# Seven block products for the queries of two cross attentions, and a value product ahead of the scores

## The reference, cut to what matters

```python
def _cross_attention(q_in, kv_in, wq, bq, wk, bk, wv, bv, wo, bo, bias_k, bias_v):
    qh = (q_in @ wq + bq).reshape(b, q_len, H, K)
    kh = (kv_in @ wk + bk).reshape(b, t, H, K)
    vh = (kv_in @ wv + bv).reshape(b, t, H, K)
    kh = jnp.concatenate([kh, broadcast(bias_k)], axis=1)
    vh = jnp.concatenate([vh, broadcast(bias_v)], axis=1)
    logits = jnp.einsum('bqhk,bthk->bhqt', qh, kh) / jnp.sqrt(K)
    weights = jax.nn.softmax(logits, axis=-1)
    ctx = jnp.einsum('bhqt,bthk->bqhk', weights, vh).reshape(b, q_len, H * K)
    return ctx @ wo + bo
# x = x + attention 1 of layer_norm(x); x = x + attention 2 of layer_norm(x); then an MLP
```

## Time and profile before

| | us |
|---|---|
| median of 3 runs | 1042.86 |
| lowest, highest | 1041.63, 1045.31 |
| the profiled execution | 1042.48 |
| its span (first to last instruction) | 1041.3 |

### The profile page before, as it was taken

How to read it: one execution, slowest core, us unless ns; L and a number is a source line. 1 busy time by engine, 2 the same in 40 slices (tenths; PEclk the granted TensorE clock), 3 DMA queues, 4 the chain that set the end, 5 groups by cost and what they waited for, 6 DMA issues and landing times.

```text
span 1041.3 us, 21141 instructions
## 1 busy us (share of the span) xinstructions
PE 1003.6 (96%) x8239; PEld 902.9 (87%) x8239; DVE 768.8 (74%) x1229; ACT 577.5 (55%) x1288; POOL 651.5 (63%) x595
## 2 busy tenths in 40 slices
PE   8899999999999999999998999999998999989998
PEld 7788888888988999999997999999998888777877
DVE  7997888998265677877668876778875387898760
ACT  5998888797533323232233322213225489999982
POOL 6885476655577475344367566655535388999960
PEclk9999999999999999999999999999999999999999
DMA  8200001000121211221121111101120000000000
GB/s 335 110 2 2 1 2 42 2 1 2 47 76 42 71 35 58 71 82 42 41 76 30 41 42 41 31 19 33 31 102 1 1 1 2 2 2 2 12 11 21
DMA packets 33931, 40.73 MB, mean 39 GB/s; under 512 B 2127, under 2 KB 31273, under 8 KB 32297
## 3 DMA queue, kind: packets, MB, share of 16 engines
q1 hardware_dynamic: 33833, 39.38, 11.3%
HBM read 38.32 MB, written 1.05 MB: 38 GB/s over the span
## 4 chain that ended last, share of the span: by engine, by line
PE 79%; POOL 9%; DVE 5%; ACT 4%; issue 1%; DMA 1%; SPq 0%; DVEq 0%; ACTq 0%; POOLq 0%
PE psum L912 10%; PE psum L791 9%; PE psum L807 9%; PE psum L992 8%; PE psum L944 8%; PE psum L926 6%; PE psum L979 5%; PE psum L958 5%; PE psum L833 5%; POOL C tile L1789 3%; PE psum L718 3%; PE psum L968 3%; PE psum L823 3%; PE psum L848 2%; POOL C tile L1795 2%; PE psum L862 1%
## 5 line engine op out<-in xcount | busy, mean ns | idle before, releaser
L1926 POOL TENSOR_TENSOR B tile<-B tile,B rec 128x1024 f32<-128x1024 f32 x32 | 61.1, 1908 | 164.5 <-DVE B rec L1348 164.5
L1795 POOL TENSOR_TENSOR A tile<-A tile,outer rec 128x1024 f32<-128x1024 f32 x48 | 91.0, 1905 | 57.9 <-DVE outer rec L1187 57.8
L1652 ACT COPY B PT<-psum 128x512 f32<-128x512 f32 x64 | 32.9, 600 | 140.7 <-PE psum L968 140.7
L1069 DVE TENSOR_SCALAR B qT<-psum,cols 128x1024 f32<-128x1024 f32 (+1 forms) x38 | 44.0, 1166 | 78.0 <-PE psum L912 76.6
L1567 ACT ACTIVATE A tile<-A tile,outer min 128x128 f32<-128x128 f32 (+1 forms) x256 | 92.3, 448 | 2.6 <-DVE outer min L1180 2.5
L1567 ACT ACTIVATE C tile<-C tile,outer min 128x128 f32<-128x128 f32 x256 | 77.8, 396 | 0.5 <-DVE outer min L1180 0.4
L944 PE MATMUL psum<-B v hi,cT hi 128*128 128x256 f32 x256 | 72.1, 282 | 0.3 <-ACT B kT L1482 0.3
L944 PE MATMUL psum<-B v hi,cT lo 128*128 128x256 f32 x256 | 71.6, 280 | 0.0
L944 PE MATMUL psum<-B v lo,cT hi 128*128 128x256 f32 x256 | 71.6, 280 | 0.0
L1795 POOL TENSOR_TENSOR C tile<-C tile,outer rec 128x1024 f32<-128x1024 f32 x32 | 60.8, 1906 | 6.1 <-DVE outer rec L1187 6.1
L1173 DVE TENSOR_TENSOR A tile<-m,psum 128x1024 f32<-128x1024 f32 x48 | 56.5, 1216 | 9.2 <-PE psum L823 8.0
(11 more groups left out here) (327 smaller groups left out, 3474.8 us busy)
## 6 DMA issues: line engine op xcount, KB each, us to landing
weights<-in_weights_c SPq DMA_DIRECT2D x5, 1024.0 KB, 6.4
raw<-in_wq SPq DMA_DIRECT2D x32, 128.0 KB, 2.7
raw<-in_wk SPq DMA_DIRECT2D x32, 128.0 KB, 3.2
raw<-in_wv SPq DMA_DIRECT2D x16, 256.0 KB, 2.8
raw<-in_wo SPq DMA_DIRECT2D x16, 256.0 KB, 2.7
weights<-in_weights_a SPq DMA_DIRECT2D x1, 3072.0 KB, 20.7
weights<-in_weights_a SPq DMA_DIRECT2D x1, 2048.0 KB, 11.5
wide<-in_bias_v SPq DMA_DIRECT2D x2, 1024.0 KB, 9.4
```

The lines of the kernel that those rows point to most:

```text
L1795: pool.tensor_tensor(tile(u, ly.nk), tile(u, ly.nk), part.rec[:, u % 4, 0:ly.per].unsqueeze(2).to_broadcast([P, ly.per, ly.nk]), ALU.mult) ...
L1926: pool.tensor_tensor(tv, tv, m.brec[:, h, :].unsqueeze(2).to_broadcast([P, B, S]), ALU.mult).then_inc(s["normalised"].sem, s["normalised"] ...
```

## The change

1. **Queries by seven products.** `in_seven`, `seven_products`, `cut_forms`, `copy_product`, `add_products`, `end_products` take the kind ("k" or "q") as an argument. The queries are made from seven products in (1, 3) to (1, 7) and (2, 2) to (2, 7): 11 turns. Their input is the normed x, which differs between j = 1 and 2, so the sums of quarters are made twice, by the same four steps: `begin_halves(j, "q")` on POOL at the end of turn 0 of each j; `end_halves(j, "q")` on DVE behind the query drains of (1, 1) and of (2, 0); `upper_halves(j, "q")` on ACT at the end of (1, 1) and (2, 0); `lower_halves(j, "q")` on POOL at the end of (1, 1) and, in (2, 1), between the divisions and the key weights.
2. **The fourth value product of both turns 0** goes ahead of the scores, on PE and DVE (for j = 1 in the orders written by hand, for j = 2 in the loop).
3. **Room.** The query sums lie where three of stage C's weights were loaded early (LATER: L3_w1, L3_w_ao, L3_w_q). Those are loaded behind the last query products, and POOL's four splits of L3_w1 (eight instructions) go from (2, 1) to (2, 4) to the end of (2, 7), ahead of clearing stage C's value tiles.
4. The scale of the queries goes from the drain into the exponential. No instruction is added by that.

```diff
-EARLY = [(0, AT_C["L2_w_fc2"]), (AT_C["L3_w_qkv"], AT_C["L3_w_q"]), (AT_C["L3_w_q"], AT_C["L3_w_co"]), (AT_C["L3_w1"], AT_C["L3_w2"])]
+LATER = [(AT_C["L3_w1"], AT_C["L3_w2"]), (AT_C["L3_w_ao"], AT_C["L3_w_q"]), (AT_C["L3_w_q"], AT_C["L3_w_kv"])]
+EARLY = [(0, AT_C["L2_w_fc2"]), (AT_C["L3_w_qkv"], AT_C["L3_w_ao"]), (AT_C["L3_w_kv"], AT_C["L3_w_co"])]
...
-def in_seven(j, turn):
-
-    return turn > 0 and (j, turn) >= (1, 3)
+FIRST_SEVEN = {("k", 1): 3, ("k", 2): 1, ("q", 1): 3, ("q", 2): 2}
+
+
+def in_seven(kind, j, turn):
+
+    return turn >= FIRST_SEVEN[kind, j]
...
     def project_pair(j, kind, turn):
-        if kind == "k" and in_seven(j, turn):
-            seven_products(j, turn)
+        if in_seven(kind, j, turn):
+            seven_products(j, kind, turn)
...
         if turn == 0:
             project_heads(j, "q", 1)
+            if j == 2:
+                values_of(2, 0, 3)
             for h in range(2):
                 scores_of(j, 0, h)
-            values_of(j, 0, 3)
             project_pair(j, "k", 1)
...
-        shared = not last and in_seven(j, turn + 1)
-        if shared:
-            add_products(j, turn + 1)
+        shared = {kind: not last and in_seven(kind, j, turn + 1) for kind in "kq"}
+        if shared["k"]:
+            add_products(j, "k", turn + 1)
         divide_by_sum(j, turn, 1)
-        if shared:
-            end_products(j, turn + 1)
+        if shared["k"]:
+            end_products(j, "k", turn + 1)
         if (j, turn) == (1, 1):
-            make_halves()
+            end_halves(1, "k")
         for n in range(4) if turn else ():
             values_of(j, turn, n)
-        if not last:
+        if shared["q"]:
+            add_products(j, "q", turn + 1)
+            end_products(j, "q", turn + 1)
+        elif not last:
             queries_of(j, 2 * turn + 2)
             queries_of(j, 2 * turn + 3)
+        if (j, turn) in ((1, 1), (2, 0)):
+            end_halves(j, "q")
         for h in range(2):
             weigh_heads(j, turn, h)
...
+        if (j, turn) == (2, 1):
+            lower_halves(2, "q")
         if turn < NP_ - 2:
             cut_pair(j, "k", turn + 2)
         elif (j, turn) == (1, NP_ - 2):
             cut_pair(2, "k", 0)
         cut_output(j, turn)
         if (j, turn) == (1, 0):
-            begin_halves()
+            begin_halves(1, "k")
+        if turn == 0:
+            begin_halves(j, "q")
         if (j, turn) == (1, 1):
-            lower_halves()
+            lower_halves(1, "k")
+            lower_halves(1, "q")
         if (j, turn) == (1, NP_ - 1):
             cut_pair(2, "q", 0)
         if j == 2 and 1 <= turn < 5:
             cut_up("M2", turn - 1)
-            cut_up("L3c", turn - 1)
...
+        if (j, turn) == (2, NP_ - 1):
+            for n in range(4):
+                cut_up("L3c", n)
```

More of the change, by code:

```diff
@@ L355, in __init__ @@
             self.kT = [s2(f"kT{k}", [P, B * S]) for k in range(2)]
[L356 to L359, removed]
+            self.cut, self.blocks = {}, {}
+            for kind in "qk":
+                self.blocks[kind] = parts(kind, [P, 4, HK])
+                for n in range(2):
+                    self.cut[f"{kind}{n}"] = [part[:, 2 * n:2 * n + 2, :] for part in self.blocks[kind]]
             self.cut["v"] = parts("v", [P, 2, 2 * HK])
@@ L722, in tensor_program, with once @@
     loaded = set()
-    def once(signal, value):
-        if signal not in loaded:
-            loaded.add(signal)
+    def once(signal, value, of=None):
+        if (signal, of) not in loaded:
+            loaded.add((signal, of))
             pe.wait_ge(s[signal].sem, value)
@@ L1315, in add_products, with end_products @@
             added.sem, added.mark((*event, "C22")))
-    def end_products(j, turn):
-        z, event, made, added = head_bank(j, "k", 2 * turn), (j, turn), s["product_made"], s["products_added"]
-        first, second = (m.col[f"L2_bk{j}"][:, 2 * turn + h:2 * turn + h + 1] for h in range(2))
-        c11, c12, c21, _ = (m.kT[k][:, n * BANK:(n + 1) * BANK] for k in range(2) for n in range(2))
+    def end_products(j, kind, turn):
+        z, event, made, added = head_bank(j, kind, 2 * turn), (j, turn), s[kind + "_product_made"], s[kind + "_products_added"]
+        first, second = (m.col[f"L2_b{kind}{j}"][:, 2 * turn + h:2 * turn + h + 1] for h in range(2))
+        c11, c12, c21, _ = (head_tile(m, kind)[k][:, n * BANK:(n + 1) * BANK] for k in range(2) for n in range(2))
         dve.wait_ge(made.sem, made.at((*event, "A22")))
@@ L1671, in scalar_program @@
             exponentials(j, turn, h)
-        if not last and in_seven(j, turn + 1):
-            copy_product(j, turn + 1)
+        if not last and in_seven("k", j, turn + 1):
+            copy_product(j, "k", turn + 1)
         elif not last:
@@ L1678, in scalar_program @@
             turn_weights(j, turn, h)
+        if not last and in_seven("q", j, turn + 1):
+            copy_product(j, "q", turn + 1)
         if last and j == 1:
@@ L1855, in cut_head, with cut_forms @@
         cut(j, f"{kind}{k}", head, (f"w{kind}_loaded{k}", 16 * ((j - 1) * NP_ + head // 2 + 1)))
-    def cut_forms(j, turn):
-        made, raw, forms, event = s["form_made"], m.k_raw, m.forms_raw, (j, turn)
+    def cut_forms(j, kind, turn):
+        made, upper, lower = s[kind + "_form_made"], s[kind + "_forms_hi"], s[kind + "_forms_lo"]
+        raw, forms, blocks, event = m.blocks_raw[kind], m.forms_raw[kind], m.blocks[kind], (j, turn)
         a21, a22, a11, a12 = (raw[:, n, :] for n in range(4))
@@ L1885, in begin_halves @@
+        pool.tensor_tensor(m.forms[kind][1][:, :, :], forms[:, :, :], m.forms[kind][0][:, :, :], ALU.subtract).then_inc(
+            lower.sem, lower.mark((*event, "made")))
+    def begin_halves(j, kind):
+        made, raw = s[kind + "_half_made"], m.halves_raw[kind]
         for name, of, (less, more), spare in (("T1", 0, ("B11", "B12"), 2), ("T3", 2, ("B12", "B22"), 3)):
             if name == "T3":
-                pool.wait_ge(made.sem, made.at("T1"))
-            pool.tensor_tensor(raw[:, of, :], m.half_of(more, 0), m.half_of(less, 0), ALU.subtract)
```

199 lines of the change are left out of this document (110 added, 89 removed).

## The result

| | before | after |
|---|---|---|
| median, us | 1042.24 (4 runs, 1040.97 to 1045.31) | 1053.06 (4 runs, 1051.50 to 1055.98) |
| the profiled execution, us | 1042.48 | 1052.38 |
| its span, us | 1041.3 | 1051.1 |
| mean granted clock of TensorE | 0.998 | 0.990 |

The ratio of after to before is 1.0097, with a 95% interval of 1.0069 to 1.0125. The kernel became 10 us slower; the forecast was 6 us slower, 1048.8 us, with a range of 1044.0 to 1054.0. The measured median lies inside that range by 0.9 us, and 1.1 us above the stretch of 1046 to 1052 that the forecast itself called its likely case.

The account below looks back on a forecast made before the run. PE, busy 96% of the span, was taken to bound ordinary turns, with POOL to watch in the first turns. Terms -8.1 + 0.4 + 1.6 (idle and clock) + 12.2 + 0.2 = +6.3 us on 1042.48 gave 1048.8 us, range 1044.0 to 1054.0.

Parts of the forecast that it names:

- The main loss (+12.2): Turns (2, 0) and (2, 1): DVE's query sums wait for POOL's T3 ahead of OT lo, delaying PE; +12.2 us.
- The gain in (1, 0) (-5.5): Turn (1, 0): the value product ahead of the scores removes PE's waits and slow clock; -5.5 us.
- The 1.7 us for the clock: Turn (1, 0): 18 matmuls behind the 2.46 us wait ran at half clock; recovering full clock was to give -1.7 us.
- POOL takes it back (+0.4 at the values of (1, 2)): Turns (1, 1) and (1, 2): POOL's query sums delay the value weights, leaving +0.4 us net up to there.
- Ordinary turns (-8.1): Eleven turns with seven query products: each was to save PE 0.74 us, in all -8.1 us.
- DVE and POOL follow (0): Ordinary turns: added work, 2.4 us on DVE and 2.7 on POOL per turn, was to be hidden; 0 us.
- Stage C (+0.2): Stage C: four moved L3c splits, 7.7 us, just hidden in POOL's 7.60 us wait for DVE; +0.2 us.
- That DVE isn't held (1): Turn (2, 0): POOL has T3 by the end of the query drains, so no hold; 1037.1 us, chance 7%.
- Smaller stalls (2): Stalls there but smaller, clock held up and POOL's waits filled by other work; 1045.5 us, chance 15%.
- DVE as the bound (3): Turns with seven query products: DVE becomes the bound and each loses its gain and more; 1057.6 us, chance 9%.
- Does DVE follow?: Ordinary turns: DVE's chain has 1.6 us slack; late by all added work less slack, it costs 0.8 us a turn.
- The contended sums (4): Sums of quarters pay full contended price on DVE, and with it POOL, 5.9 us more; 1054.7 us, chance 6%.

Follow-up runs that it names:

- Experiment 1: Changed kernel with the j = 2 query sums' DVE, ACT and POOL lower-part steps one turn later, seven query products from turn 3; 1040.94 us, ratio 0.9979.
- experiment 5: Changed kernel with POOL's T1 and T3 of (2, 0) right behind the divisions, ahead of key and output weights; 1049.24 us, ratio 1.0062.
- experiment 6: Changed kernel with DVE's four query sums of (2, 0) behind OT lo in place of ahead of it; 1050.95 us, ratio 1.0068.
- experiment 2: Kernel before with only the fourth value product of both turns 0 moved ahead of the scores, all queries plain; 1036.42 us, ratio 0.9940.
- Experiment 3: Changed kernel with the fourth value products put back behind the scores, nothing else undone; 1055.01 us, ratio 1.0115.
- Experiment 4: Changed kernel with POOL's lower parts of the j = 1 query sums moved to (1, 2), between value weights and divisions; 1049.61 us, ratio 1.0059.
- experiment 7: Changed kernel with the moves of experiments 1 and 4, plus j = 1 query T1 and T3 behind the divisions of (1, 1); 1032.14 us, ratio 0.9899.
- experiment 8: Kernel of experiment 7 with the j = 1 lower parts at the end of (1, 2), query products from turn 4; 1030.60 us, ratio 0.9882.

## Why the prediction was right, and where it was short

**The main loss (+12.2): right in place, mechanism and size.** It said that PE would start the output projection at 597.7 and the query products of (2, 1) at 617.7; they started at 596.83 and 617.42. From the scores of (1, 7) to these query products it was 90.04 us (605.53 - 515.49) and is 102.37 (617.42 - 515.05): +12.3. DVE's idle time was to be 11 us and was 11.58. In part small errors cancelled: T3 ended 0.9 us before its forecast, and the step from DVE's first maximum to the second reciprocal took 13.6 us in place of 13.1. Experiment 1 takes the hold away and gets 12.3 us back. Experiments 5 and 6 shorten it and get 3.6 and 3.0.

**The gain in (1, 0) (-5.5): measured -5.7 in the step from scores to scores, -6.3 with (2, 0) by experiment 2.** The 1.7 us for the clock in it was no sure gain. Experiment 3 has the same 2.46 us wait at full clock, and five of 24 runs of the kernel before show a mean clock of 1.000, so it doesn't pay it in every execution either.

**POOL takes it back (+0.4 at the values of (1, 2)): right, 0.7 us short.** Forecast were waits of 1.5 and 3.3 us, measured 3.08 and 4.19. POOL's value weights came at 342.8 and 377.6 in place of 342.0 and 377.0, and PE was 6.4 us early in place of 5.5. The step that was short is POOL's plain split of the query weights in (1, 1), taken at the 2.3 us that it had before. It now stands beside DVE's sums of the key quarters and took 340.84 - 336.94 = 3.9 us; T1 of the keys had begun 0.8 us earlier than reckoned, which leaves the value weights 0.8 us late. PE then reaches (1, 2) 3.3 us early and not 4.0, and all that follows there comes 0.6 to 0.7 later. First and fifth instruction of that stretch on POOL, and one of DVE's sums beside it:

```profile
336.94 0.86 POOL L1880 CAST B q hi<-raw 128x256 fp32r<-128x256 f32 x1
...
340.84 0.60 POOL L1880 CAST B v hi<-raw 128x512 fp32r<-128x512 f32 x1
```

```profile
338.38 1.12 DVE L1357 TENSOR_TENSOR weights<-cT hi,weights 128x512 f32<-128x512 f32 x1
```

One stretch of half clock followed the second wait, and from the first value matmul to the transposing it took 384.88 - 377.68 = 7.20 us in place of 382.29 - 376.63 = 5.66: 1.5, forecast 1.6. Its window, columns as in the earlier trace rows:

```profile
380.00:382.00 2.00, 2.00 (x11) 2.00 (x11) 0.61 (x1) 0.00 (x0) 2.00 (x3) 0.50 0.00 0
```

Experiment 4 takes the second wait away.

**Ordinary turns (-8.1): the sign right, the size short by 1.4.** A turn with seven query products lasts 29.99 us in place of 30.60, 0.61 saved and not 0.74. This term of the sum was mis-sized because the 4.83 us were read from the key products, which stand behind the output projection. The queries stand behind the transposing, and there the first matmul steps on by 0.32 us, in both kernels:

```profile
416.55 0.48 PE L946 MATMUL psum<-B hT hi,B q hi 128*128 128x512 f32 x1
416.87 0.40 PE L946 MATMUL psum<-B hT lo,B q hi 128*128 128x512 f32 x1
417.10 0.40 PE L946 MATMUL psum<-B hT hi,B q lo 128*128 128x512 f32 x1
...
421.50 3.74 PE L999 MATMUL psum<-B PT,B v 128*128 128x128 f32 x32
```

The 21 matmuls take 421.50 - 416.55 = 4.95 us. A cost that stands once in a block doesn't shrink with the number of its instructions: only 3 x 0.23 was to be had, less what the slightly slower step costs.

**DVE and POOL follow (0): right.** The query products for (1, 3) start at 386.55, behind the transposing of (1, 2); the scores that need them start at 395.08, 8.5 us later, with no wait (the forecast had 8.4). POOL waited 7.78 us for DVE ahead of the first division of (1, 4), and now 3.60; the next one keeps its 4 us. These are the rows before and after:

```profile
433.20 1.90 POOL L1926 TENSOR_TENSOR B tile<-B tile,B rec 128x1024 f32<-128x1024 f32 x1 [7.78 <-DVE B rec L1348]
```

```profile
434.58 1.90 POOL L1964 TENSOR_TENSOR B tile<-B tile,B rec 128x1024 f32<-128x1024 f32 x1 [3.60 <-DVE B rec L1369]
440.46 1.90 POOL L1964 TENSOR_TENSOR B tile<-B tile,B rec 128x1024 f32<-128x1024 f32 x1 [3.98 <-DVE B rec L1369]
```

**Stage C (+0.2): the work was hidden, the time came out at +1.4.** POOL's first wait of 7.60 us is filled by the four splits, so that the same instruction now follows with no wait before it, and PE waits for POOL there as little as before:

```profile
803.16 0.70 POOL L1745 TENSOR_TENSOR outer rstd<-outer ve,half 128x2 f32<-128x2 f32 x1
```

The 1.4 us go with two stretches of half clock at 914 to 918 and 934 to 939, for example

```profile
916.00:918.00 2.00, 2.00 (x7) 1.65 (x7) 1.47 (x2) 1.73 (x6) 1.58 (x2) 0.53 0.00 0
```

They don't come with the moved splits. From the scores of (2, 7) to the end the kernel before needs 273.8 us and the changed one 275.2. Experiment 2, with POOL's splits at their old place, has two such stretches as well and needs 275.5. Of the kernels with the splits moved, those of experiments 1, 6, 7 and 8 have none and need 273.1 to 273.4, those of experiments 3, 4 and 5 have one and need 274.6.

So of the 3.5 us by which the sum was short, 1.4 belong to the turns, 0.7 to POOL's slowed query weights in (1, 1), which PE pays in (1, 2), and 1.2 to stage C and its clock. The rest, 0.2, is within what two executions differ by. That the clock would fall in stage C was in no term; the number would have come out nearer in an execution without it.

**The rivals.** That DVE isn't held (1) fell in the first trace. Smaller stalls (2) fell too: 10.3, 4.2 and 3.1 us. DVE as the bound (3) fell, since turns of 29.99 us have no wait for it; its price of 1057.6 counts 0.8 us a turn, as worked out under "Does DVE follow?", though its sentence names the 0.74 besides. The contended sums (4): in (2, 0) DVE's four took 0.93, 0.83, 0.82 and 0.87 us, 3.5 in all where 3.2 was taken and 9.1 was the upper bound. Most of the price was POOL's, whose query sums of 128 x 128 beside them took 0.90 us in place of 0.46; there nobody waited for it, but in (1, 1) the 1.6 us that POOL lost reached PE. So this rival was right about the contention, but the full price on DVE wasn't paid. The Trainium skill, GPSIMD Engine Reference, section 1 (Specifications), says that POOL shares its SBUF interfaces with VectorE and that they contend when a DVE instruction has two SBUF inputs; the trace agrees.

## What to carry to other kernels

A one-off step that waits for another engine belongs where nothing that PE wants stands behind it in its queue; here such steps cost 20.6 us more at one place than at another, a turn later or behind the divisions (the one turn of query products given up for it is inside that number). Add up the chain to the instruction at which it meets another engine's queue, not to the wait that PE shows: the wait can be taken away for 3 us where it reads 10. A saving is to be read from the block that it changes, not from its neighbour, since what stands ahead of a block can change the cost of its first matmul (0.32 us behind the transposing, 0.23 behind the output projection).

## What the runs showed of the hardware

**The clock falls behind some waits and not behind others of the same length.** The wait of 2.46 us in (1, 0) was followed by half clock in the profile of the kernel before and not in that of experiment 3; the wait of 2.2 us for bank 5 in (2, 0) wasn't followed by it before, and was in experiment 3 (571 to 576 us). The wait of 3.08 us in (1, 1), with the same instructions ahead of it, was followed by half clock in experiments 1, 4 and 5 (turns of 35.91 to 36.04 us) and not in the changed kernel and experiment 6 (34.41 us). The loss is 1.5 us each time in (1, 0) and (1, 1). The Trainium skill, TensorE: Matmul & The Clock Gate, Part 1, says that the gate runs by a time of its own and varies from run to run; the trace agrees. The spread of this kernel goes with it: of 24 runs of the kernel before on one chip, the five with a mean granted clock of 1.000 took 1040.06 to 1040.93 us, the four with 0.998 took 1041.14 to 1042.16, and the ten with 0.995 took 1043.90 to 1047.98. Where a difference of a few us matters, the mean clock of each run belongs beside its time.

**DVE's sums of two SBUF tiles and POOL's instructions slow each other, and who pays changes from place to place.** In (2, 0) DVE's four sums took 0.82 to 0.93 us, where the same four took 0.68 to 0.69 at the end of (1, 1) with POOL standing still, and POOL's 128 x 128 instructions beside them went from 0.46 to 0.90. In experiment 5 that was 1.8 us of POOL's time, and PE waited for it. In other places it was DVE that paid: 2.27 us for one sum in the earlier trace rows, 1.72 for one at the end of (1, 1) in experiment 7. What decides who pays no run here shows.
